# The first group's node work and turn moved from the expert stage into the last attention step

## The chip, the cores and the metric

The kernel runs on one core of one Trainium2 chip. The metric is the device time of one execution in microseconds (us), as the median of several runs; smaller is better. The core has a matrix engine (TensorE, PE in the rows), VectorE (DVE), ScalarE (ACT), GpSimd (POOL) and SyncE (SP), which run side by side and wait for each other through semaphores. SP only issues DMAs here; GpSimd issues the indirect gathers of the attention.

## The reference, cut to what matters

```python
xn = _layernorm(x, axis=-1)                     # 6250 nodes, 256 columns
x = x + relu(gat(xn, edges)) + mix(xn)          # 200000 edges sorted by destination, and a linear attention
x = x + ffn(_layernorm(x, axis=-1))             # 8 experts of three 256x256 layers, router weights w

# gat, for a node: alpha = exp(e - max) / sum, out = sum(alpha * xp[src]) over its edges, 4 heads of 64
# mix, for a node: v + q2 kv / sqrt(N), with q2 divided by its sum and its norm (a reciprocal and a root)
# ffn:
h = relu(bn(xn2 @ W1[e])); h = relu(bn(h @ W2[e])); y[e] = h @ Wo[e] + bo[e]; out = sum_e w[:, e] * y[e]
```

All of it is in float32. Between the two halves stands, for each node, what this text calls the **node work**: divide the sums of the edge attention by their denominator, take the relu, add x and the mix term with its own scale, take mean and variance, normalize. The normalized rows are then turned (transposed), since the experts' products need the columns on the partitions.

## The kernel before

The 6250 nodes lie in 49 blocks of 128, and the blocks in 7 groups of 7 (`IB = 7`). Three stages follow each other, each in an `nc.Block()`, at whose end all engines wait for each other: `prepare`, `attend`, `experts`.

**attend** goes through the edge list in 55 steps of up to 8 visits (the last has 7). A visit is 512 gathered edges with one block of destinations. In a step VectorE first works out the running maxima and the factors of the whole step (a long chain of small instructions, with TensorE turns and small products between), ScalarE takes the exponentials `fo` and `w`, and then the visits run. In visit v VectorE makes `y` (L1300, three quarters of it; ScalarE the fourth, L920), TensorE multiplies it by the one-hot matrix into `ps_y` (L1068), and VectorE scales the running sums `acc` (L1437) and adds `ps_y` (L1442) one visit later. ScalarE widens the one-hot matrix to float32 (L979). Between the visits VectorE builds the one-hot matrices of the next step (L1164); in the last step there is nothing to build, and `first_scales` (nine small instructions) and `first_bases` (x and the mix term of the first group, seven instructions, L1358) stand there. The rows of mix for the first group come by a DMA (`first_in`, L825) that SP issues one step before the end. GpSimd's part of attend ends with the last gather.

**experts** goes through 7 groups and in each through 8 experts. For an expert, TensorE makes two hidden layers (L1598, into `ps_h`, which ScalarE takes out, L1651) and the output (L1608), which VectorE adds up with the router's weight (L1818). The node work of group g+1 runs on VectorE between the experts of group g. The first group has no group before it: its node work, `first_nodes` (L1672 to L1690), stands at the stage's start on VectorE, in two halves, with turns on TensorE (`turns`, L1573) and copies on ScalarE (`turned`, L1632) behind it, and the first hidden layer's products stand behind those. At the stage's start SP issues the loads of the experts' weights (L1545, three of 256 KB for each expert), then `bo`, the router's rows and the mix rows of the second group. TensorE's first hidden product waits for the first expert's three loads.

The order on each engine is the order of the code, which is written out for each engine apart; there is no planner. A semaphore's count is held from one stage to the next, so work that is moved to attend has to raise the counts that experts waits for.

Each of the engines' programs takes its instructions in order: a wait holds up all that stands behind it on that engine.

## Time and profile before

| | us |
|---|---|
| median of 3 runs | 4544.69 (4532.37 to 4567.01) |
| profiled execution | 4539.39, of which the span is 4537.6 |
| attend ends, experts begins (from the span's start) | 3498.3 |
| TensorE busy over the span | 3066.3 (68%) |
| VectorE | 2271.5 (50%) |
| ScalarE | 1537.3 (34%) |
| GpSimd | 1500.8 (33%) |

The times in the rows further down are in us from the span's start. The profiled execution ran 5.3 us below the median of the runs. The stage `experts` takes the last 1039 us of the span, the stage `attend` most of what lies before it. The change touches some 50 us around the border between the two, so the profile is read there, instruction by instruction. Busy time of TensorE is modelled at its ends, and GpSimd's spans are rough.

### The profile page before, as it was taken

Reading aid. Unit: us, or ns where it says so; the run is one execution under the profiler, and the core shown is the slowest. Engines: PE = TensorE matmul, PEld = TensorE weight load, DVE = VectorE, ACT = ScalarE, POOL = GpSimd, SP = SyncE. Lnnn points to the kernel's source line nnn. Section 1 sums busy time; section 2 is a strip of 40 time slices with the busy share of each in tenths; the row PEclk is TensorE's granted clock in tenths of the full one; section 3 lists DMA queues with packets and bytes.
Section 4 is the critical chain, followed back from the end, with each engine's and each line's share of the span. In section 5 each row is a group of like instructions: output and inputs, shape, how many; then the busy total and the mean of one; then the engine's idle time right before and its main releaser. Section 6 shows DMA issues by size and latency. Waiting matters only on the chain. (4 is left out here: it accounts for less than half of the span.)

```text
span 4537.6 us, 61951 instructions
## 1 busy us (share of the span) xinstructions
PE 3066.3 (68%) x18597; PEld 2300.7 (51%) x18597; DVE 2271.5 (50%) x6618; ACT 1537.3 (34%) x4071; POOL 1500.8 (33%) x1622
## 2 busy tenths in 40 slices
PE   6365655565545556665665555555657999999999
PEld 4244544454434455554554444444545666666665
DVE  5154544554544544444444454454547666666653
ACT  3033333333332333333333333333334333333333
POOL 0545444444444444434444343444441000000000
PEclk8577766776766677777777776776767999999999
DMA  6323222322222223322333222222222110101100
GB/s 221 98 73 84 75 79 73 82 76 79 70 74 73 68 82 88 82 77 76 87 82 90 70 71 66 72 75 72 74 73 86 52 33 25 33 9 33 30 11 9
DMA packets 203310, 315.96 MB, mean 70 GB/s; under 512 B 77409, under 2 KB 137442, under 8 KB 202850
## 3 DMA queue, kind: packets, MB, share of 16 engines
q0 software_dynamic: 75360, 212.42, 17.6%
q1 hardware_dynamic: 118722, 90.76, 6.7%
q10 hardware_dynamic: 8896, 8.82, 0.6%
q8 instruction: 151, 2.47, 0.2%
q14 instruction: 181, 1.48, 0.1%
HBM read 279.51 MB, written 26.86 MB: 68 GB/s over the span
## 5 line engine op out<-in xcount | busy, mean ns | idle before, releaser
L768 POOL DMA_INDIRECT xg<-edge_table,idx x1564 | 1485.5, 950 | 1810.1 <-ACT y L920 823.9
L1068 PE MATMUL ps_y<-y,hotw 128*128 128x260 f32 x3512 | 1036.2, 460 | 830.2 <-DVE y L1300 655.9
L1068 PEld LDWEIGHTS ps_y<-y,hotw 128*128 128x128 f32 x3512 | 793.6, 233 | 1048.7 <-ACT hotw L979 677.1
L1442 DVE TENSOR_TENSOR acc<-acc,ps_y 128x260 f32 x439 | 186.8, 425 | 1244.5 <-remote 986.3
L979 ACT CAST hotw<-hot 128x512 f32<-128x512 bf16 x439 | 265.8, 620 | 1041.4 <-remote 701.8
L920 ACT ACTIVATE y<-xg,w 128x65 f32 x1756 | 463.5, 337 | 9.0 <-issue 1.6
L870 ACT COPY hot_t<-ps_o 128x1024 bf16<-128x1024 bf16 x220 | 213.2, 1014 | 652.1 <-remote 486.7
L1300 DVE TENSOR_TENSOR y<-xg,ps_v 128x780 f32<-128x780 f32 x439 | 417.0, 960 | 8.5
L1818 DVE SCALAR_TENSOR_TENSOR xg<-ps_ye,wts,xg 128x256 f32<-128x256 f32 x392 | 189.7, 484 | 400.0 <-PE ps_ye L1608 399.8
L1608 PE MATMUL ps_ye<-wo,xg 128*128 128x256 f32 x1568 | 352.5, 382 | 0.5 <-DVE xg L1818 0.5
L1598 PE MATMUL ps_h<-xg,w 128*128 128x448 f32 x896 | 348.3, 542 | 1.0 <-issue 0.5
L1598 PE MATMUL ps_h<-tables,w 128*128 128x448 f32 x896 | 345.9, 539 | 0.0
L1651 ACT ACTIVATE tables<-ps_h,bnb,bns 128x448 f32<-128x448 f32 x224 | 162.3, 724 | 494.9 <-PE ps_h L1598 494.9
L1608 PEld LDWEIGHTS ps_ye<-wo,xg 128*128 128x128 f32 x1568 | 280.1, 189 | 81.3 <-DVE xg L1818 12.9
L1164 DVE TENSOR_TENSOR hot<-ps_v,tables 128x1024 bf16<-128x1024 f32 x220 | 263.1, 1217 | 0.0
L1598 PEld LDWEIGHTS ps_h<-tables,w 128*128 128x128 f32 x896 | 170.2, 190 | 166.5 <-issue 124.9
L1598 PEld LDWEIGHTS ps_h<-xg,w 128*128 128x128 f32 x896 | 171.0, 191 | 150.9 <-issue 126.9
L1651 ACT ACTIVATE xg<-ps_h,bnb,bns 128x448 f32<-128x448 f32 x224 | 162.3, 724 | 174.5 <-PE ps_h L1598 174.5
L1437 DVE TENSOR_TENSOR acc<-acc,ps_v 128x260 f32 x439 | 182.8, 416 | 0.1
L1051 PE MATMUL ps_fml<-pair,hot_t 128*128 128x8 bf16 x5280 | 147.5, 176 | 41.9 <-ACT hot_t L870 41.9
L1051 PEld LDWEIGHTS ps_fml<-pair,hot_t 128*128 128x128 bf16 x5280 | 147.6, 101 | 46.5 <-ACT hot_t L870 46.5
L1035 PE MATMUL ps_fml<-tail,hot 128*128 128x13 bf16 x1760 | 56.1, 172 | 167.6 <-DVE tail L1222 153.3
(289 smaller groups left out, 3410.5 us busy)
## 6 DMA issues: line engine op xcount, KB each, us to landing
xg<-edge_table,idx POOLq DMA_INDIRECT x1564
mix_rows<-kk SPq DMA_DIRECT2D x49, 257.0 KB
xg<-mix_rows SPq DMA_DIRECT2D x7, 1799.0 KB, 7.9
xb<-in_xt SPq DMA_DIRECT2D x50, 128.0 KB
xnk<-in_x SPq DMA_DIRECT2D x50, 128.0 KB
x<-in_x SPq DMA_DIRECT2D x7, 896.0 KB, 12.4
xt<-in_xt SPq DMA_DIRECT2D x7, 896.0 KB, 9.4
xb<-in_xt SPq DMA_DIRECT2D x24, 256.0 KB
```

The lines of the kernel that those rows point to most:

```text
L768: pool.indirect_dma_start(xg[:, q * OCT + u, j, :], None, dr["table"], bass.IndirectOffsetOnAxis(ap=idx[q][:, c:c + 1], axis=0)).then_inc( ...
L870: act.copy(hot_t[:, 2 * p:2 * p + 2, :].rearrange("p v n -> p (v n)"), ps_o[p % 2][:]).then_inc(ht_d, 1)
L920: mul = act.activation(y[v % 2][:, YV, at], xg[:, bass.ds(slot[v], 1), YV, at].rearrange("p o c -> p (o c)"), ACT.Copy, scale=w[:, v * CH ...
L979: act.copy(hotw[v % 2][:], hot[q][:, v, :, :]).then_inc(hotw_d, 1)
L1051: mm = pe.matmul(ps_l[:, c * 8:c * 8 + 8], hot_t[:, v, j * P:(j + 1) * P], pair[:, k, :, v], start=(k == 0), stop=(k == 2))
L1068: mm = pe.matmul(ps_y[v % 2][:, 0:RW], hotw[v % 2][:, j, :], y[v % 2][:, j, :], start=(j == 0), stop=(j == CH - 1))
L1164: dve.tensor_tensor(hot[q][:, part * k:(part + 1) * k, :, :].rearrange("p v j n -> p (v j) n"), bc(iota, 1, k * CH), bc(rel, 2, P), ALU.is ...
L1300: dve.tensor_tensor(y[v % 2][:, 0:YV].rearrange("p j (h c) -> p j h c", c=HC), xg[:, bass.ds(slot[v], 1), 0:YV, 0:RW].rearrange("p o j (h ...
L1598: mm = pe.matmul(ps_h[g % 4][:, 0:HN], wl[:, kh, e, mh * P:(mh + 1) * P], src[:, kh, half * HN:(half + 1) * HN], start=(kh == 0), stop=(kh ...
L1608: mm = pe.matmul(ps_y[j % 2][:, 0:D], h2[:, kh, j * P:(j + 1) * P], wo[:, kh, e, :], start=(kh == 0), stop=(kh == 1))
L1651: act.activation((h1, h2)[layer][:, mh, half * HN:(half + 1) * HN], ps_h[g % 4][:, 0:HN], ACT.Relu, bias=K.bnb[:, layer, c:c + 1], scale=K ...
L1818: dve.scalar_tensor_tensor(yb[q][:, j, :], ps_y[j % 2][:, 0:D], wts[q][:, j, e:e + 1], yb[q][:, j, :], ALU.mult, ALU.add).then_inc(S["expe ...
```

## The change

The node work of the first group and its turn are moved into the last step of attend and divided anew:

- GpSimd takes, behind its last gather, one product (sums by denominators), the relu, two sums and the product of the mix term, each over all seven blocks at once (128 x 1792), and later the seven normalizations (128 x 256).
- VectorE gives it the reciprocals of the denominators at the step's start, has `first_scales` ahead of the visits' factors instead of in visit 1, loses the seven `first_bases`, and takes the statistics of the seven blocks in visit 3, their variances in visit 4 and the last reciprocal in visit 6.
- ScalarE takes the first root ahead of the exponential `w` and the second in visit 5, and copies the turned rows behind its visits.
- TensorE turns the seven blocks behind its seven visits, into banks of attend.
- `first_nodes`, `turns` and `turned` go from experts. GpSimd raises the counts for them.
- Some buffers change their place in the gather ring, and the small results get a room there.

```diff
@@ gpsimd, behind the last gather
+                for name in ("z_done", "gat_done", "stats_done_e", "aggr_done_e", "zn_done", "node_products", "node_reads"):
+                    pool.sem_inc(K.exp[name], IB)
+                pool.sem_inc(K.exp["den_done"], 1)
+
+                pool.wait_ge(fsh_d, ONE + 1)
+                pool.wait_ge(y_d, ONE + FREE * SV)
+                pool.wait_ge(ya_d, ONE + FREE * SV)
+                x2 = K.yb[0]
+                pool.tensor_tensor(x2.rearrange("p j (h c) -> p j h c", c=HD),
+                                   K.acc[:, 0:IB, 0:RW].rearrange("p j (h c) -> p j h c", c=HC)[:, :, :, 0:HD],
+                                   bc(f_den, 3, HD), ALU.mult).then_inc(fsum_d, 1)
+                pool.wait_ge(fsum_d, ONE + 1)
+                pool.tensor_scalar(x2, x2, 0.0, None, ALU.max).then_inc(fsum_d, 1)
+                pool.wait_ge(fsum_d, ONE + 2)
+                pool.wait_ge(first_in, 16)
+                pool.tensor_tensor(x2, x2, K.t7[:, :, D + 2:MW], ALU.add).then_inc(fsum_d, 1)
+                pool.wait_ge(fq3_d, ONE + 3)
+                pool.tensor_tensor(temp, K.t7[:, :, 0:D], bc(small[:, 5, :], 2, D), ALU.mult).then_inc(fsum_d, 1)
+                pool.wait_ge(fsum_d, ONE + 4)
+                pool.tensor_tensor(x2, x2, temp, ALU.add).then_inc(fsum_d, 1)
+                pool.wait_ge(frs_d, ONE + 1)
+                for j in range(IB):
+                    pool.tensor_scalar(K.x7[:, :, j, :], x2[:, j, :].rearrange("p (k c) -> p k c", c=P), f_mv[:, j, 0:1], f_std[:, j:j + 1],
+                                       ALU.subtract, ALU.mult).then_inc(fzn_d, 1)
@@ scalar, last step, between the exponentials fo and w
+                    if n(1) == NS - 1:
+                        act.wait_ge(first_in, 16)
+                        act.activation(small[:, 2, :].unsqueeze(2), K.t7[:, :, D + 1:D + 2], ACT.Sqrt).then_inc(froot_d, 1)
@@ scalar, in the visits
-                        if v == 0 and n(1) == NS - 1:
-                            act.wait_ge(first_in, 16)
-                            act.activation(small[:, 2, :].unsqueeze(2), K.t7[:, :, D + 1:D + 2], ACT.Sqrt).then_inc(froot_d, 1)
+                        if v == 5 and n(1) == NS - 1:
+                            act.wait_ge(fvar_d, ONE + 1)
+                            act.activation(f_std, f_std, ACT.Sqrt).then_inc(fstd_d, 1)
@@ scalar, behind the steps
+                for j in range(IB):
+                    act.wait_ge(ftn_d, ONE + j + 1)
+                    act.copy(K.zt[0][:, :, j * P:(j + 1) * P], (ps_t, ps_q)[j % 2][:, 0:D].rearrange("p (k n) -> p k n", n=P)).then_inc(fzt_d, 1)
@@ tensor, behind the steps
+                pe.wait_ge(mixc_d, ONE + NB)
+                pe.wait_ge(fmax_d, ONE + NS)
+                for j in range(IB):
+                    pe.wait_ge(fzn_d, ONE + j + 1)
+                    pe.wait_ge(fzt_d, ONE + max(j - 1, 0))
+                    for kh in range(2):
+                        mm = pe.transpose((ps_t, ps_q)[j % 2][:, kh * P:(kh + 1) * P], K.x7[:, kh, j, :], ident)
+                    mm.then_inc(ftn_d, 1)
@@ vector, last step, behind the reading of the running maxima
+                    if n(1) == NS - 1:
+                        dve.reciprocal(f_den.unsqueeze(3), K.acc[:, 0:IB, 0:RW].rearrange("p j (h c) -> p j h c", c=HC)[:, :, :, HD:HC]).then_inc(fsh_d, 1)
@@ vector, ahead of the look-up
                     if n(1) < NS - 1:
                         build(2, *nxt)
+                    else:
+                        first_scales()
@@ vector, in the visits
-                        elif v == 1:
-                            first_scales()
-                            first_bases(0, 3)
-                        elif v == 2 and n(1) == NS - 1:
-                            first_bases(3, 5)
                         elif v == 3 and n(1) == NS - 1:
-                            first_bases(5, IB)
+                            first_stats()
+                        elif v == 4 and n(1) == NS - 1:
+                            first_vars()
+                        elif v == 6 and n(1) == NS - 1:
+                            first_norms()
@@ vector, new functions
+                def first_stats():
+
+                    dve.wait_ge(fsum_d, ONE + 5)
+                    for j in range(IB):
+                        dve.bn_stats(f_stats[:, j, :], K.yb[0][:, j, :]).then_inc(fst_d, 1)
+
+                def first_vars():
+                    dve.wait_ge(fst_d, ONE + IB)
+                    for j in range(IB):
+                        dve.bn_aggr(f_mv[:, j, :], f_stats[:, j, :]).then_inc(fag_d, 1)
+                    dve.wait_ge(fag_d, ONE + IB)
+                    dve.tensor_scalar(f_std.unsqueeze(2), f_mv[:, :, 1:2], LN_EPS, None, ALU.add).then_inc(fvar_d, 1)
+
+                def first_norms():
+                    dve.wait_ge(fstd_d, ONE + 1)
+                    dve.reciprocal(f_std, f_std).then_inc(frs_d, 1)
@@ experts, tensor
-                    if first:
-                        turns(q, t, 0, HALF)
-                    elif e == 0:
+                    if e == 0 and not first:
                         pe.wait_ge(S["turned"], ONE + t(1))
...
-                            if first and layer == 0:
-                                if half == 1:
-                                    turns(q, t, HALF, IB)
-                                pe.wait_ge(S["node_reads"], ONE + (IB if half else HALF))
@@ buffers
-            K.zt = [room((2 + q) * IB * D, 2 * IN_, "p (k n) -> p k n", n=IN_) for q in range(2)]
-            K.h2 = room(4 * IB * D, 2 * IN_, "p (k n) -> p k n", n=IN_)
+            free = NG % RING * CH * TW
+            K.zt = [room(at, 2 * IN_, "p (k n) -> p k n", n=IN_) for at in (free, 3 * IB * D)]
+            K.h2 = room(2 * IB * D, 2 * IN_, "p (k n) -> p k n", n=IN_)
+            K.fr = ring[:, free + 2 * IN_:free + 2 * IN_ + 13 * IB]
```

How the instructions stand on three engines, before and now. Line numbers differ between the two, since lines were added. VectorE in the last step, from the saving of the maxima to visit 3, before (`sc` are the scores, `small_a` the first group's scales, `xg` in L1358 the group's bases):

```order
L1283 TENSOR_TENSOR sc<-asrc,ps_fml 128x128
L1285 SCALAR_TENSOR_TENSOR sc<-sc 128x128
L1287 TENSOR_TENSOR sc<-sc,ps_fml 128x128
L1289 TENSOR_SCALAR sc<-sc 128x128
L1291 COPY ps_v<-fo 128x32
L1293 COPY ps_v<-w 128x128
...
L1352 TENSOR_TENSOR small_a<-small_a 128x7
L1358 SCALAR_TENSOR_TENSOR xg<-xg,small_a 128x256 x3
L1437 ISA
L1437 TENSOR_TENSOR acc<-acc,ps_v 128x260
L1442 TENSOR_TENSOR acc<-acc,ps_y 128x260
```

VectorE there now:

```order
L1398 TENSOR_TENSOR small_a<-small_a 128x7
L1330 TENSOR_TENSOR sc<-asrc,ps_fml 128x128
L1332 SCALAR_TENSOR_TENSOR sc<-sc 128x128
...
L1405 BN_STATS xg<-xg 128x6 x7
L1494 ISA
L1494 TENSOR_TENSOR acc<-acc,ps_v 128x260
L1499 TENSOR_TENSOR acc<-acc,ps_y 128x260
L1347 ISA
L1347 TENSOR_TENSOR y<-xg,ps_v 128x780
L1410 BN_AGGR xg<-xg 128x2 x7
L1412 TENSOR_SCALAR xg<-xg 128x7
```

The scales stand ahead of the scores now, and statistics and variances stand between a visit's `y` and the adding up of the visit before.

ScalarE from the exponential `fo` (L937) to `w` (L944), now:

```order
L937 ACTIVATE fo<-zz 128x32
L940 ACT_TABLE_LOAD
L940 ACTIVATE small_a<-xg 128x7
L944 ACT_TABLE_LOAD
L944 ACTIVATE w<-sc 128x128
```

The root stands between the two exponentials with a table load on either side; before, it stood behind `w` and the first visit's `y`, with one load.

GpSimd from its last gather to its stage's end, now (before, the last gather was followed by the end):

```order
L773 DMA xg<-edge_table,idx 128x264 x4
L794 ISA
L794 TENSOR_TENSOR xg<-acc,xg 128x1792
L798 TENSOR_SCALAR xg<-xg 128x1792
L801 TENSOR_TENSOR xg<-xg 128x1792
L803 TENSOR_TENSOR xg<-xg,small_a 128x1792
L805 TENSOR_TENSOR xg<-xg 128x1792
L808 TENSOR_SCALAR xg<-xg 128x2x128 x7
```

## Rows read from the trace of the kernel before

**Rows 1.** Windows: start:end, length, busy us (instructions) by engine, PEclk, DMA share, GB/s.
```profile
3530.00:4500.00 970.00, 969.47 (x3210) 592.42 (x3209) 574.31 (x1787) 326.28 (x455) 0.00 (x0) 1.00 0.08 22
```

**Rows 2.** Timeline of PE: start, length, line, operation, count, idle before and its releaser.
```profile
3506.34 2.24 PE L1573 MATMUL ps_n<-cst,xg 128*128 128x128 f32 x8 [8.85 <-DVE xg L1690]
3509.09 5.32 PE L1598 MATMUL ps_h<-xg,w 128*128 128x448 f32 x8 [0.51 <-issue]
...
3519.50 6.18 PE L1598 MATMUL ps_h<-tables,w 128*128 128x448 f32 x16
```

**Rows 3.** Timeline of DVE at the end of attend and the start of experts.
```profile
3497.60 0.43 DVE L1442 TENSOR_TENSOR acc<-acc,ps_y 128x260 f32 x1 [0.77 <-PE ps_y L1068]
3498.35 0.33 DVE L1672 RECIPROCAL den<-acc 128x28 f32<-128x28 f32 x1 [0.33 <-PEq L746]
...
3503.83 0.38 DVE L1681 BATCH_NORM_AGGREGATE mv_e<-stats_e 128x2 f32<-128x6 f32 x4
...
3505.78 1.38 DVE L1690 TENSOR_SCALAR xg<-xg,mv_e,small 128x256 f32<-128x256 f32 x4
```

**Rows 4.** Issues by SP, and times to landing of the last load and of L825.
```profile
3462.33 0.38 SPq L825 DMA_DIRECT2D xg<-mix_rows  x1
...
3499.67 0.60 SPq L1545 DMA_DIRECT2D wo<-in_wo  x1
...
wo<-in_wo SPq DMA_DIRECT2D x1, 256.0 KB, 5.5
...
DMA to landing us min/median/max: 7.4/7.4/7.4
```

**Rows 5.** Windows around the border, the granted clock before the DMA share.
```profile
3512.00:3513.00 1.00, 1.00 (x3) 0.38 (x2) 0.00 (x0) 0.55 (x1) 0.00 (x0) 0.50 1.09 347
3513.00:3516.00 3.00, 2.28 (x10) 1.19 (x8) 0.00 (x0) 1.48 (x5) 0.00 (x0) 0.95 1.10 349
```

**Rows 6.** Timeline of DVE in the last step.
```profile
3472.03 0.26 DVE L1232 TENSOR_REDUCE zz<-ps_fml 128x32 f32<-128x96 f32 x1 [1.13 <-PE ps_fml L1035]
...
3474.33 1.38 DVE L1248 TENSOR_SCALAR acc<-st 128x4 f32 x7
3478.26 0.38 DVE L1283 TENSOR_TENSOR sc<-asrc,ps_fml 128x128 f32<-128x128 f32 x1 [2.55 <-PE ps_fml L1051]
...
3480.37 1.84 DVE L1300 TENSOR_TENSOR y<-xg,ps_v 128x780 f32<-128x780 f32 x2
3482.14 0.16 DVE L1335 TENSOR_TENSOR small_a<-rs 128x7 f32<-128x7 f32 x1
...
3484.01 1.28 DVE L1358 SCALAR_TENSOR_TENSOR xg<-xg,small_a 128x256 f32<-128x256 f32 x3
```

**Rows 7.** Timeline of ACT in the last step, and of its first copies in experts.
```profile
3475.96 0.23 ACT L908 ACTIVATE fo<-zz 128x32 f32<-128x32 f32 x1
...
3481.11 1.28 ACT L935 ACT_TABLE_LOAD   x1
...
3507.04 0.80 ACT L1632 COPY xg<-ps_n 128x256 f32<-128x256 f32 x2 [2.38 <-PE ps_n L1573]
```

**Rows 8.** Timeline of DVE in the step before: first y, and the seventh adding up.
```profile
3446.78 1.84 DVE L1300 TENSOR_TENSOR y<-xg,ps_v 128x780 f32<-128x780 f32 x2
...
3462.43 0.43 DVE L1442 TENSOR_TENSOR acc<-acc,ps_y 128x260 f32 x1
```

**Rows 9.** Groups of POOL: line, operation, count, busy us, mean ns, idle before.
```profile
L750 POOL CAST idx<-ix 128x32 int32<-128x32 int16 x49 | 10.9, 222 | 78.0 <-POOLq L111 77.9
...
L246 POOL MEMSET acc<- 128x196 f32 x1 | 0.4, 445 | 0.3 <-POOLq L1924 0.3
```

**Rows 10.** Timeline of POOL: the last gather of the program.
```profile
3417.27 0.95 POOL L768 DMA_INDIRECT xg<-edge_table,idx  x1 [0.30 <-issue]
```

**Rows 11.** Single lines of DVE: count, shortest, median and longest ns, first and last start.
```profile
L1218 DVE TENSOR_TENSOR tails<-tails,tail x55: 291/293/294, 230.9 to 3470.0; 128x128 f32<-128x128 f32 x55
L1289 DVE TENSOR_SCALAR sc<-sc x55: 226/226/228, 241.8 to 3479.3; 128x128 f32<-128x128 f32 x55
```

More of the change, by code:

```diff
@@ L697, in attend @@
          k_d, kb_d, k2_d, kr1_d, kr_d, kn_d, ka_d, kas_d, col_d, one_d, root_d, kv_d, kvs_d, lim_d, rec_d, kv1_d,
-         fq1_d, fq2_d, froot_d, fq3_d, base_d, dg_d) = (K.att[n] for n in ATTEND_COUNTS)
+         fq1_d, fq2_d, froot_d, fq3_d, dg_d,
+         fsh_d, fsum_d, fst_d, fag_d, fvar_d, fstd_d, frs_d, fzn_d, ftn_d, fzt_d) = (K.att[n] for n in ATTEND_COUNTS)
         YV = CH - 1
@@ L1353, in first_scales @@
                     dve.wait_ge(fq3_d, ONE + 3)
-                def first_bases(lo, hi):
-                    for j in range(lo, hi):
-                        dve.scalar_tensor_tensor(K.yb[0][:, j, :], K.t7[:, j, 0:D], small[:, 5, j:j + 1], K.t7[:, j, D + 2:MW],
-                                                 ALU.mult, ALU.add).then_inc(base_d, 1)
+                def first_stats():
[11 more added lines that the diff above has]
+                    dve.reciprocal(f_std, f_std).then_inc(frs_d, 1)
                 def bias(p):
@@ L1614, in _ @@
             def _(act):
-                def product(k, j, t):
-                    act.wait_ge(S["node_products"], ONE + t(NPR) + ((k - 3) * IB + j + 1))
                 def node(k, q, t, before):
@@ L1627, in node @@
                         act.activation(lg[:], lg[:], ACT.Exp).then_inc(S["lg_exp"], 1)
-                def turned(q, t, lo, hi):
-                    for j in range(lo, hi):
-                        product(3, j, t)
-                        act.copy(zt[q][:, :, j * P:(j + 1) * P], ps_n[j % 2][:, 0:D].rearrange("p (k n) -> p k n", n=P)).then_inc(S["node_reads"], 1)
                 def expert(e, q, t):
@@ L1636, in expert @@
                     first = e == 0 and t(1) == 0
-                    if first:
-                        for k, at in enumerate((slice(0, HALF), slice(HALF, IB))):
-                            act.wait_ge(S["half_var"], ONE + k + 1)
-                            act.activation(small[:, 9, at], small[:, 8, at], ACT.Sqrt).then_inc(S["half_std"], 1)
-                            if k == 0:
-                                turned(q, t, 0, HALF)
                     for layer in range(2):
                         for half in range(2):
-                            if first and layer == 0 and half == 1:
-                                turned(q, t, HALF, IB)
                             for mh in range(2):
@@ L1808, in expert @@
                     if e == 0 and t(1) == 0:
-                        first_nodes(q, t)
                         first_weights(q, t)
```

45 lines of the change are left out of this document (7 added, 38 removed).

## The prediction, written before the changed kernel ran

> **What bounds the kernel now.** I began with the windows. Behind 3530 us TensorE is busy for 969.5 of 970 us at full clock [rows 1]: the expert stage is TensorE's, it has no slack, and whatever moves its first products moves the end by the same amount. So the whole question is when TensorE gets through its opening. The timeline of TensorE shows that opening [rows 2]: the visits end at 3497.5, the engine is idle for 8.85 us, turns four blocks, starts on the first hidden layer at 3509.09, stops once more for the other three blocks, and begins the second hidden layer at 3519.50. From there it does not stop for the first group's node work again. I use 3519.50 as the mark: what the second layer's start gains or loses, the kernel gains or loses. VectorE's timeline shows what fills the hole [rows 3]: the stage border at 3498.3, then the node work, whose first normalized blocks come from 3505.8 on.
>
> Two other things are hidden in that hole. The first expert's third load is issued at 3499.67 and takes 5.5 us [rows 4], so it lands at about 3505.2, 6.9 us behind the border. Now nothing waits for it, since the products come at 3509.09. And the granted clock is still 0.50 (1.2 GHz) up to 3513, then 0.95 and full (2.4 GHz) [rows 5]; after the idle stretch it is low for 6.7 us, counted from TensorE's restart at 3506.34.
>
> **What experts saves.** With the first group turned in advance, the first product waits for the weights alone. Loads can't be issued ahead of the border, as their room belongs to experts, so it starts 7.0 us behind it. It saves no more than the time from there. The first layer has 16 products. At the low clock one takes 0.77 us (5 of them in the 3.9 us from 3509.09 to 3513), at full clock 6.18 / 16 = 0.386 us [rows 2]. TensorE is idle for those 7 us again, so I carry the 6.7 us at the low clock over: 8.7 products in them, and 7.3 more in 2.8 us, together 9.5 us. The second layer starts 7.1 + 9.5 = 16.6 us behind the border. Before it was 3519.5 - 3498.3 = 21.2. **Saved: 4.6 us.** With a border later than 3502.9 the change loses.
>
> **What the last step of attend costs.** From front to back:
> - The reciprocal of the denominators takes 0.33 us [rows 3] on VectorE ahead of the scan L1209, on the chain. That chain meets slack at the look-up, which TensorE's own queue holds up (VectorE waits 2.55 us for it ahead of 3478.26).
> - `first_scales` takes 1.9 us (3482.14 to 3484.01) and goes into that wait, which begins at 3475.7 [rows 6]. Its sixth instruction needs the root. ScalarE ends `fo` at 3476.2 [rows 7], loads a table in 1.28 us and has the root at 3477.8; four more instructions end at 3478.6. The scores start at 3478.65, **0.4 us later**. The second table load (1.28 us) fits before `w`, which is due at 3480. Behind ScalarE's new wait for `first_in` stand `w` and all visits, but that DMA is issued at 3462.3 and lands 7.4 us later, at 3469.7 [rows 4], so it holds nothing.
> - Out of the visits go the scales (1.9 us) and the bases (seven at the pitch of L1358, 1.28 us for three, 3.0 us) [rows 6]. The step before shows visits without these. From the first `y` to the seventh adding up 3462.43 - 3446.78 = 15.65 us [rows 8]; in the last step it is 3497.60 - 3480.37 = 17.2 [rows 3, 6]. The builds that stand in that step are covered by TensorE's slow first visit.
> - Into the visits come seven statistics at the pitch of a 128x256 instruction, 0.35 us (1.38 us for 4 of L1690) [rows 3], 2.5 us; seven aggregates and a small one (0.38 us for 4) [rows 3], 1.0 us; a reciprocal, 0.2 us. From visit 2 on the visits run at 1.75 us with VectorE, TensorE and ScalarE all near full, so I count all 3.7. ScalarE's root in visit 5 costs 1.5 us with its table load, ahead of the last widening; I take 0.4 of it as showing, between none and all. The last adding up then starts at 3480.8 + 15.65 + 3.7 + 0.4 = 3500.5, and TensorE ends its visits with it.
> - GpSimd. Its last gather starts at 3417.27 [rows 10], so the count raising and the library's reload lie in 45 us of idleness; at nothing, as long as the reload is shorter. It starts at about 3467, when the denominators are there. No row shows a GpSimd instruction of this kind. Below: VectorE's rate, about 2.1 us for 1792 elements (780 in 0.92) [rows 8]. Above: GpSimd's own slope, (445 - 222) ns over (196 - 32) elements = 1.36 ns each [rows 9], once for each of two inputs, 5.05 us. One input by that slope is 2.6 us. For two I take 3.8, the middle between one pass and two of the engine's own rows. Four of 3.8 and one of 2.6: the first three run from 3467 to 3477.3, the other two from the scales at 3478.7 to 3486.4. VectorE comes to its statistics behind `y` of visit 3, at 3480.8 + 8.1 = 3488.9. So **no wait, with 2.5 us to spare**; at 5.05 us it would wait 1.1 us. Behind that wait stand the scaling and adding of visit 2 and `y` of visit 4, so TensorE would stand too.
> - The normalizations begin at about 3498.2, seven of 0.53 us (0.18 + 256 x 1.36 ns) end at 3501.9, in time for the turns. TensorE's seven turns start at 3500.5 and go at the pitch of the copies, 0.5 us (two in 0.80, and a short wait for the next turn) [rows 7], and the last copy ends at 3504.3. The border is 0.3 us later, at **3504.6**. Nothing is behind these on the three engines but the border itself, for which SP's weight loads wait.
>
> Sum: 3504.6 - 3502.9 = **+1.7 us**. The changed places of the buffers cost nothing; shapes and engines are the same. The mix rows of the second group come behind all weight loads and so 6.3 us later too; ScalarE takes their root ahead of the second expert's results, and TensorE can fill four banks of hidden products (6 us) meanwhile, so a wait of that size does not reach it.
>
> Against the profiled execution that is 4539.4 + 1.7 = 4541.1. The median of the runs lies 5.3 us above the profiled one, and a new median should as well: **4546**.
>
> **The rivals.**
>
> *The two engines share a way to SBUF* and VectorE's instructions with two inputs there wait for a whole GpSimd instruction. For it: in the last step the engines would now work side by side on SBUF for the first time. Against it: L1218 (two inputs in SBUF) took 291 to 294 ns and L1289 226 to 228 in all 55 steps, under gathers or not [rows 11]; but a gather reads little more than indices. Price: L1218, due at 3470.3, waits for the first product to end at 3470.75, the next two for the relu (3473.65) and the sum (3477.7). L1232 then comes at 3479.1 instead of 3472.03 and the scales end at 3484.7. The square of the scores (L1285) waits behind GpSimd's fourth to 3488.6, and L1289 behind the fifth to 3492.7. `y` starts at 3493.8, 13 us later than in my sum. That makes 4554 on the profiled one and **4559** on the median; with only the first half of it, 4551. The Trainium skill, "SBUF — State Buffer", section "Who interferes with whom", says that a VectorE instruction with two SBUF inputs, or in a two-port mode, and a GpSimd instruction that reads SBUF exclude each other for the whole instruction. By that rule, this is what happens.
>
> *GpSimd is at the cheap end* (2.1 us), ScalarE's root is hidden and half of the statistics falls into slack of the visits: the border is at 3502.5, the kernel 0.4 us faster; with a shorter stretch at the low clock 2 to 3 us faster, **4542**. It can't be more, since the weights' landing stands behind the border.
>
> *The library's reload is long*: slower. Place: the row ahead of GpSimd's first product. It decides from about 48 us on, the gap from 3419 to 3467; above that each us holds the statistics, VectorE and TensorE. No row prices it. At 100 us it would add some 54, **4600**. If it is paid instead at the first product, with some us, it adds what goes over the 2.5 to spare, 4 or 5. For that the Trainium skill, "GPSIMD Engine Reference", section "2.1 Instruction dispatch", gives about 6 us for the first call of a freshly loaded kernel; no run here shows it.
>
> **Chances.** My sum 0.42; the shared way, whole or in part, 0.38; the cheap end 0.12; the reload exposed 0.08, of which 0.03 above 45 us. The runs scattered from 4532 to 4567, so a median of a few can lie 10 us off without any change. The range takes in the cheap end less this, and the shared way plus this: 4532 to 4569. A measurement of this kernel tells about 1%, 45 us, from no change. No case but a long reload reaches that: faster by over 1% 0.01, within 0.96, slower 0.03.
>
> **What would show it.** In the changed profile: (1) the border near 3504.6, and the first hidden product 7 us behind it, waiting for a DMA; (2) no wait of VectorE for GpSimd in visit 3, the GpSimd products near 3.8 us; (3) L1218 and its like at 0.29 us, and the scores at 3478.7; if they stretch to the ends of GpSimd's instructions, the rival is right; (4) GpSimd's first product at 3467; (5) the turns at 0.5 us each behind the visits; (6) the first layer in about 9.5 us. Wrong would make it above all (3), and a GpSimd instruction above 5 us.

## The result, and the profile after

| | before | changed |
|---|---|---|
| median of the runs taken in turn, us | 4553.1 (4532.37 to 4567.01, 14 runs) | 4583.66 (4568.44 to 4592.8, 14 runs) |
| profiled execution, us | 4539.39 | 4576.59 |
| its span, us | 4537.6 | 4574.8 |

The ratio is 1.0061, with a 95% interval of 1.0046 to 1.0075: **the kernel became some 30 us slower** (21 to 34 by the interval). Within the 1% that counts here as no change, but outside the predicted range of 4532 to 4569, and 38 us above the predicted 4546. Of these 38, 8.4 are no part of the change: the 14 runs of the kernel before have their median at 4553.1, where the three runs ahead of the prediction had 4544.7.

All comparisons below count from one instruction that stands in every version: the scan `fmax` (`TENSOR_TENSOR_SCAN`) of the last attention step. Up to it the kernels run the same code but for the reciprocals of the denominators (0.32 us on VectorE, just ahead of it), and yet the profiled executions on comparable chips reach it at 3459 to 3484 us, in no order that goes with the edits (before 3466.52, and 3468.32 when profiled again; changed 3479.82; experiment 6 below 3483.91, experiment 8 3459.11). I take that as scatter of the 54 steps ahead, and so 13.3 of the 37.2 us between the two spans; no run shows it apart from a small cost of the change up there. The rest lies behind the scan:

| us behind the scan | before | changed | predicted |
|---|---|---|---|
| first `y` of the visits | 13.85 | 28.27 | 14.3 |
| last adding up starts | 31.08 | 47.00 | 34.0 |
| last copy of the turns ends | (in experts) | 54.52 | 37.8 |
| border (SP's first weight issue) | 31.79 | 62.86 | 38.1 |
| first hidden product | 42.57 | 68.26 | 45.1 |
| second hidden layer (the mark) | 52.98 | 75.89 | 54.7 |

(The predicted column is the prediction's own times less 3466.52.) The mark is 22.9 us later instead of 1.7. Another 0.95 us is lost behind it, and from there to the end nothing: 13.3 + 22.9 + 0.95 = 37.2.

The timeline of VectorE of the changed kernel, last step (start, length, line, operation, count, idle before and its releaser), answers to [rows 6, 11]:

```profile
3479.82 1.19 DVE L1254 TENSOR_TENSOR_SCAN fmax<-seg_step,ps_at 32x512 f32<-32x512 f32 x1
3482.03 0.72 DVE L1259 TENSOR_TENSOR tail<-ps_fml,tables 128x128 bf16<-128x128 f32 x1 [1.02 <-PE ps_fml L1058]
...
3483.09 0.29 DVE L1263 TENSOR_TENSOR tails<-tails,tail 128x128 f32<-128x128 f32 x1
3483.41 4.68 DVE L1265 CAST tail<-tails 128x128 bf16<-128x128 f32 x1
3488.13 3.73 DVE L1267 TENSOR_TENSOR tail<-tails,tail 128x128 bf16<-128x128 f32 x1
...
3499.08 0.17 DVE L1392 TENSOR_TENSOR small_a<-small_a 128x7 f32<-128x7 f32 x1 [1.28 <-ACT small_a L940]
...
3500.34 2.95 DVE L1332 SCALAR_TENSOR_TENSOR sc<-sc 128x128 f32<-128x128 f32 x1
...
3503.65 3.61 DVE L1336 TENSOR_SCALAR sc<-sc 128x128 f32<-128x128 f32 x1
...
3508.09 1.84 DVE L1347 TENSOR_TENSOR y<-xg,ps_v 128x780 f32<-128x780 f32 x2
...
3526.82 0.43 DVE L1499 TENSOR_TENSOR acc<-acc,ps_y 128x260 f32 x1 [0.77 <-PE ps_y L1103]
```

And GpSimd's own timeline beside it, whole from its last gather on:

```profile
3479.96 3.19 POOL L794 TENSOR_TENSOR xg<-acc,xg 128x1792 f32<-128x1792 f32 x1 [45.05 <-DVE xg L1247]
3483.24 4.74 POOL L798 TENSOR_SCALAR xg<-xg 128x1792 f32<-128x1792 f32 x1
3488.07 3.61 POOL L801 TENSOR_TENSOR xg<-xg 128x1792 f32<-128x1792 f32 x1
3499.97 3.18 POOL L803 TENSOR_TENSOR xg<-xg,small_a 128x1792 f32<-128x1792 f32 x1 [8.29 <-DVE small_a L1398]
3503.23 3.96 POOL L805 TENSOR_TENSOR xg<-xg 128x1792 f32<-128x1792 f32 x1
3524.75 8.44 POOL L808 TENSOR_SCALAR xg<-xg 128x256 f32<-128x256 f32 x7 [17.56 <-DVE xg L1416]
```

Lay the two over each other. L1265 starts 0.17 us behind the start of GpSimd's L798 and ends with it, at 3488.0 to 3488.1; L1267 ends with L801; L1332 with L803; L1336 (L1289 of before, 226 ns in all 55 steps there) with L805. Nobody is named as releaser: the time is inside the instruction. L1263 (L1218 of before), which starts 0.06 us before L794 ends and runs across the gap of 0.09 us to L798, keeps its 0.29, and L1259, which reads one input from PSUM, runs at 0.72 in the middle of L794. L1265, L1267 and L1332 are L1220, L1222 and L1285 of before, where they took, in all 55 steps (count, shortest/median/longest ns, first and last start):

```profile
L1220 DVE CAST tail<-tails x55: 245/249/316, 231.3 to 3470.3; 128x128 bf16<-128x128 f32 x55
L1222 DVE TENSOR_TENSOR tail<-tails,tail x55: 316/319/327, 231.5 to 3470.6; 128x128 bf16<-128x128 f32 x55
L1285 DVE SCALAR_TENSOR_TENSOR sc<-sc x55: 291/291/294, 241.1 to 3478.7; 128x128 f32<-128x128 f32 x55
```

The turns, on TensorE, and what stands behind them; answers to [rows 2]:

```profile
3526.55 0.38 PE L1190 MATMUL ps_at<-cst,xg 128*128 128x128 f32 x2
...
3533.25 0.69 PE L1190 MATMUL ps_at<-cst,xg 128*128 128x128 f32 x2 [0.51 <-POOL xg L808]
3548.08 7.79 PE L1640 MATMUL ps_h<-xg,w 128*128 128x448 f32 x16 [14.14 <-DMA wo<-in_wo]
3555.71 6.18 PE L1640 MATMUL ps_h<-tables,w 128*128 128x448 f32 x16
3561.73 3.19 PE L1621 MATMUL ps_n<-wr,xg 128*128 128x8 f32 x28
3564.77 8.02 PE L1650 MATMUL ps_ye<-wo,xg 128*128 128x256 f32 x28
3572.63 6.18 PE L1640 MATMUL ps_h<-xg,w 128*128 128x448 f32 x16
```

ScalarE's last copy:

```profile
3533.97 0.37 ACT L1024 COPY xg<-ps_at 128x256 f32<-128x256 f32 x1 [0.83 <-PE ps_at L1190]
```

SP's first issues behind the border; they answer to [rows 4]:

```profile
3542.68 1.31 SPq L1601 DMA_DIRECT2D w<-in_w  x2
3544.05 1.07 SPq L1601 DMA_DIRECT2D wo<-in_wo  x1
```

Between 3534.3, where the last copy ends, and 3542.68 no engine shows any work. The view of the single line that ends the stage names the one that is not done. Of the changed kernel, GpSimd and the engine that works last (count, shortest/median/longest ns, first and last start):

```profile
L751 POOLq DRAIN  x1: 17419/17419/17419, 3524.7 to 3524.7; - x1
L751 ACTq DRAIN  x1: 401/401/401, 3534.0 to 3534.0; - x1
```

The same view of the kernel before:

```profile
L746 POOLq DRAIN  x1: 8879/8879/8879, 3424.3 to 3424.3; - x1
```

At the end of a stage each engine has a row called DRAIN, and the border comes when the last of these has ended; I call it the engine's emptying, after its name. GpSimd's starts with its normalizations and lasts until 3542.1, 8.9 us behind the end of the last of them (3533.2). In the kernel before a DRAIN of 8.88 us stood at 3424.3, behind the last gather, and ended 65 us ahead of the border.

### The profile page after: what moved, and what is told of

It reads as the page before. It is cut to its first block and busy times, and to the rows that moved or that the text cites. A ratio compares the mean times of both kernels' runs of the same rounds, so it can differ in the third digit from the quotient of the medians.

```text
span 4574.8 us, 61952 instructions
## 1 busy us (share of the span) xinstructions
PE 3065.1 (67%) x18597; PEld 2302.1 (50%) x18597; DVE 2274.0 (50%) x6588; ACT 1540.6 (34%) x4072; POOL 1527.6 (33%) x1634
## 5 line engine op out<-in xcount | busy, mean ns | idle before, releaser
L1086 PE MATMUL ps_fml<-pair,hot_t 128*128 128x8 bf16 x5280 | 147.7, 175 | 45.1 <-ACT hot_t L899 41.8
L1799 DVE SCALAR_TENSOR_TENSOR xg<-bo,wts,xg 128x256 f32<-128x256 f32 x392 | 160.1, 480 | 3.6
```

What stands on the lines that cost most here:

```text
L1086: mm = pe.matmul(ps_l[:, c * 8:c * 8 + 8], hot_t[:, v, j * P:(j + 1) * P], pair[:, k, :, v], start=(k == 0), stop=(k == 2))
```

## The experiments

**The theory (A)**: three things, each with its place, make the loss behind the scan. (1) VectorE's instructions that need the way to SBUF which GpSimd uses wait for whole GpSimd operations, and ScalarE's root moves in behind them; (2) GpSimd normalizes at 1.21 us a block, so the turns follow it; (3) GpSimd's DRAIN costs about 9 us behind its last instruction. **The rival (B)** differs by experiment: the two engines slow each other by sharing a rate, whatever the size of the operations (2); the DRAIN costs its 9 us each time, or because of the computing ahead of it (1, 4, 8); part of the loss sits in the regrouped work itself, beside the weights and the clock (6). That a semaphore orders the wait is a fourth, which 2 can tell as well.

The first four runs fell on a chip that takes 3203.4 us for the kernel before; its steps of attention are shorter. Each has its own comparison there, the kernel before was timed there but not profiled, and the offsets from the scan are what is compared with the table above.

**1. GpSimd emptied early.** The changed kernel, with one line more:

```diff
@@ gpsimd, behind the counts raised for experts
+                pool.drain()
```

> The changed kernel with one drain more on GpSimd, right behind its last gather, where the engine is idle anyway; the one at the stage's end stays. The mark is the stretch from the scan of the last step (32x512) to the start of the first expert's second hidden layer: 53.0 us before, 75.9 us changed. In the changed kernel 8.3 us of it lie between the last copy of a turned block and SP's first weight load, while GpSimd's closing drain runs. Theory A (the drain works off what the gathers left, once, whenever it comes): the closing drain falls from 8.9 us behind GpSimd's last instruction to under 0.5 us, the border follows the last copy by about 0.3 us, the mark falls to 67.6 us and the time by about 8 us. Theory B (GpSimd's drain costs 9 us each time, or costs it because of the computing instructions ahead of it): the early drain shows 9 us in idleness, the closing one 9 us again, the mark stays at 76.

Measured: 3222.53 us, ratio 1.0058 (1.0041 to 1.0075). The view of the new line:

```profile
L790 POOLq DRAIN  x1: 8883/8883/8883, 2122.3 to 2122.3; - x1
```

The row that changes GpSimd's configuration, and its first product:

```profile
L795 POOLq MODIFY_POOL_CONFIG  x2: 11/11/11, 2131.3 to 2131.3; - x2
```

```profile
2131.45 3.19 POOL L795 TENSOR_TENSOR xg<-acc,xg 128x1792 f32<-128x1792 f32 x1 [15.95 <-issue]
```

ScalarE's last copy:

```profile
2187.06 0.37 ACT L1025 COPY xg<-ps_at 128x256 f32<-128x256 f32 x1 [0.83 <-PE ps_at L1191]
```

SP's first weight issue:

```profile
2187.72 1.31 SPq L1602 DMA_DIRECT2D w<-in_w  x2
```

The border comes 0.66 us behind the start of the last copy; in the changed kernel it was 8.71. So (3) holds, and a second DRAIN with no gather since the first is short: it ends 0.1 us behind the last normalization. But the mark is at 72.1, not at 67.6: on this chip the early DRAIN ends at 2131.2, 1.9 us *behind* the scan, the first product starts 2 us late, and one more of VectorE's instructions (L1264 there, 2.19 us instead of 0.29) falls into it; first `y` is 2.2 us later than in the changed kernel. The visits take 1.4 us more, for which this trace names no reason, and the weights 0.8 more. An emptying in front of due work is no gift: it took 8.1 us off the border, and the mark gained 3.8.

**2. GpSimd's long operations in pieces.** The five operations of 128x1792 become seven of 128x256 each, the rest of the changed kernel the same:

```diff
-                pool.tensor_scalar(x2, x2, 0.0, None, ALU.max).then_inc(fsum_d, 1)
+                for j in range(IB):
+                    op = pool.tensor_scalar(x2[:, j, :], x2[:, j, :], 0.0, None, ALU.max)
+                op.then_inc(fsum_d, 1)
...
```

(shown for the maximum with zero; the other four operations likewise.)

> The changed kernel with each of GpSimd's five instructions of 128x1792 cut into seven of 128x256, block by block. Theory A (a VectorE instruction that needs the shared way to SBUF waits for the whole GpSimd instruction that holds it): the stretched VectorE instructions (cast of the tails 4.68 us, the next 3.73, square of the scores 2.95, minimum of the scores 3.61) fall to at most about 1 us each, more of them are stretched a little, and the way from the scan to the first y falls from 28.3 us to about 17 to 20 (13.9 before). Theory B (the two engines slow each other by sharing bandwidth, whatever the size of the instructions): the stretched instructions stay as long in sum, some 15 us over their lengths of before, and the way stays near 28 us. GpSimd's sum may grow by some us of overhead, from 18.7 to 20 to 25.

Measured, one execution (3221.0 us): first `y` at 17.77, last adding up at 35.92, the mark at 66.7. VectorE's timeline of this kernel, the instructions that had stretched:

```profile
2137.28 0.54 DVE L1275 CAST tail<-tails 128x128 bf16<-128x128 f32 x1
2137.86 0.53 DVE L1277 TENSOR_TENSOR tail<-tails,tail 128x128 bf16<-128x128 f32 x1
...
2143.08 3.20 DVE L1303 TENSOR_SCALAR acc<-st 128x4 f32 x7
...
2149.44 0.39 DVE L1342 SCALAR_TENSOR_TENSOR sc<-sc 128x128 f32<-128x128 f32 x1
```

4.68 us became 0.54, 3.73 became 0.53, 2.95 became 0.39, and the last, 3.61, became 0.23: VectorE still waits, but for the rest of a piece of 0.6 to 0.8 us. GpSimd works no less (23.3 us for the five against 18.7), its semaphores rise at the same places, and `y` comes 10.5 us earlier. So it is (1): a shared rate, or a wait for a semaphore, would have cost as much with pieces. What is left, 3.9 us to the kernel before, is made of many small waits: seven short savings (L1303) take 3.20 us where they took 1.39.

**3. The normalizations on VectorE**, behind its last adding up, the rest of the changed kernel the same:

```diff
@@ gpsimd
-                for j in range(IB):
-                    pool.tensor_scalar(K.x7[:, :, j, :], x2[:, j, :].rearrange("p (k c) -> p k c", c=P), f_mv[:, j, 0:1], f_std[:, j:j + 1],
-                                       ALU.subtract, ALU.mult).then_inc(fzn_d, 1)
@@ vector, behind the visits
+                dve.wait_ge(frs_d, ONE + 1)
+                for j in range(IB):
+                    dve.tensor_scalar(K.x7[:, :, j, :], K.yb[0][:, j, :].rearrange("p (k c) -> p k c", c=P), f_mv[:, j, 0:1], f_std[:, j:j + 1],
+                                      ALU.subtract, ALU.mult).then_inc(fzn_d, 1)
```

> The changed kernel with the seven normalizations (128x256) on VectorE, behind its last adding up, in place of GpSimd's 1.21 us each. VectorE takes 0.35 us each (2.4 us). GpSimd's last instruction is then the second sum, at the end of the scores, so that its closing drain of 9 us lies beside the visits. Expected if both readings are right: from the last adding up to the border 2.4 + 0.8 + 0.3 = 3.5 to 4.5 us instead of 15.9, the mark 75.9 - 12 = 64 us. If the drain's length were set by the border and not by GpSimd's last instruction, the border would still come 9 us late and the mark would be 72.

Measured, one execution (3218.3 us): VectorE needs 2.34 us for the seven where GpSimd needed 8.44:

```profile
2179.39 2.34 DVE L1512 TENSOR_SCALAR xg<-xg 128x256 f32<-128x256 f32 x7
```

The border is 5.0 us behind the start of the last adding up instead of 15.9 (3.5 to 4.5 were expected), the mark at 64.8. Two causes went with one edit: the last copy came 2.8 us sooner behind the last adding up (2), and as GpSimd now ended with its fifth operation, its DRAIN lay beside the visits (3): it ends 8.9 us behind that operation and 15 us ahead of the border. The first `y` stayed at 28.0, as nothing of (1) was touched.

**4. One late instruction in the kernel before.** The reverse test of (3): nothing of the change, only a fill of one column on GpSimd that waits for the last but one adding up.

```diff
+                pool.wait_ge(acc_d, ONE + NG + NX - 1)
+                pool.memset(late[:], 0.0).then_inc(late_d, 1)
```

> The kernel before with nothing but one GpSimd memset of 128x1 more, that waits for the last but one adding up of the last step. Theory A (GpSimd's closing drain takes 9 us from its last instruction on, whatever that is, once gathers have run in the stage): the border comes about 8 us later than before, the mark rises from 53.0 to 61 us, the time by 8 us (0.2%). Theory B (only the reloaded library or the long computing instructions make the drain slow): the mark stays at 53.

Measured: 3211.11 us, ratio 1.0021 (1.0012 to 1.0031). On GpSimd's timeline:

```profile
2157.97 0.10 POOL L783 MEMSET late<- 128x1 f32 x1 [43.56 <-DVE acc L1445]
```

And on SP's:

```profile
2167.23 1.31 SPq L1548 DMA_DIRECT2D w<-in_w  x2
```

With a fill of 0.10 us the border stands 38.5 us behind the scan instead of 31.8, and from the fill's end to the border pass 9.2 us. It costs some 7 us of the kernel (0.21% of 3203), as the trace says (mark 60.0 against 53.0). The 31.8 and 53.0 are from the other chip; as the first `y` is 0.6 us earlier in this trace, the true step is perhaps that much larger.

**5. The kernel before, profiled again** on the chip of this run and the next three, where the kernel before takes about what it took in the first runs (4541.1 us here), to see how firm the offsets are:

> The kernel before, unchanged, on the chip of this call: a measure of how much of the marks is the chip's and the run's. Both theories expect the last step to take what it took in the trace shown (first y 13.9 us behind the scan, last add 31.1, first weight issue 31.8, second layer of the first expert 53.0), within 1 us, whatever the earlier steps take.

First `y` 13.79, last adding up 31.00, border 31.71, mark 52.93: all within 0.1 us of the first trace, while the scan itself stood 1.8 us elsewhere.

**6. All three suspects gone at once**: experiments 1, 2 and 3 in one kernel.

> The changed kernel with all three suspects taken away at once: GpSimd's five long operations in seven pieces each, its closing drain preceded by one behind the last gather, and the seven normalizations on VectorE behind its last add. Theory A (the loss is whole GpSimd operations held against VectorE, the normalizations on GpSimd, and the closing drain, and nothing else): first y at 17.8 us behind the scan, or up to 2 us more where the early drain ends after the scan; last add at 36 to 38; first weight issue 4.5 to 5 us behind the last add; second layer at 53 to 56 us behind the scan, where the kernel before has 53.0: a ratio of 1.000 to 1.001. Theory B (part of the loss is in the regrouped work itself, beside the experts' weights and the clock): these three gone, the mark stays at 58 us or more and the ratio at 1.0015 or more.

Measured: 4549.01 us, ratio 1.0007 (0.9989 to 1.0025). First `y` 17.73, last adding up 36.11, border 41.11, mark 54.41. Theory A's numbers, one by one. The mark is 1.4 us behind that of before: the three are the loss (21.5 of the 22.9 us), and without them the change still buys nothing. The border costs 9.3 us more (3.9 for pieces that still hold VectorE, 1.2 for the statistics in the visits, 4.3 for normalizing and turning behind them), and the experts give 7.9 back.

**7. A version meant to beat both**, from the kernel before. GpSimd keeps the sums, with its one-input operation given to ScalarE; what needs the shared way longest stands beside the visits, whose instructions on VectorE read one input from PSUM; statistics, normalizations and turns stay behind the border, where the weights are awaited anyway:

```diff
@@ gpsimd, behind its last gather
+                pool.drain()
+                pool.wait_ge(fsh_d, ONE + 1)
...
+                pool.tensor_tensor(x2..., K.acc..., bc(f_den, 3, HD), ALU.mult).then_inc(fsum_d, 1)
+                pool.wait_ge(fsum_d, ONE + 2)
...
+                pool.wait_ge(fq3_d, ONE + 3)
+                pool.tensor_tensor(x2, x2, K.t7[:, :, D + 2:MW], ALU.add).then_inc(fsum_d, 1)
+                pool.tensor_tensor(temp, K.t7[:, :, 0:D], bc(small[:, 5, :], 2, D), ALU.mult).then_inc(fsum_d, 1)
+                pool.wait_ge(fsum_d, ONE + 4)
+                pool.tensor_tensor(x2, x2, temp, ALU.add).then_inc(fsum_d, 1)
@@ scalar, last step
+                        act.wait_ge(fsum_d, ONE + 1)
+                        act.activation(K.yb[0]..., K.yb[0]..., ACT.Relu).then_inc(fsum_d, 1)
@@ vector, visits
-                            first_bases(0, 3)
...
@@ vector, first_nodes of experts
-                        dve.scalar_tensor_tensor(yb[q][:, j, :], q7[:, j, :], 0.0, yb[q][:, j, :], ALU.max, ALU.add).then_inc(S["z_done"], 1)
```

> A version meant to beat both: from the kernel before, with the node sums of the first group on GpSimd but without its long one-input operation (one product of 1792 columns at the scan, the maximum with zero on ScalarE in its idle time, three more operations beside VectorE's visits), the early drain behind the last gather, and only statistics, variances, normalizations and turns left behind the border, where the weights take 5 to 7 us to land anyway. Theory A: first y 14 to 15 us behind the scan, visits 1.5 us shorter than before, border at 30 to 32 us, second layer at 46 to 49 us against 53.0 before: 4 to 7 us gained, a ratio of 0.998 to 0.9988 here. Theory B (the three GpSimd operations beside the visits hold VectorE's products up as they held the tails, about 3 us each): border at 38 or more, and no gain.

Measured: 4536.04 us, ratio 0.9989 (0.9974 to 1.0004). First `y` 13.66, last adding up 29.60, border 30.31, mark 46.89. GpSimd's timeline:

```profile
3477.61 3.18 POOL L792 TENSOR_TENSOR xg<-acc,xg 128x1792 f32<-128x1792 f32 x1 [48.74 <-DVE xg L1228]
3494.91 3.62 POOL L798 TENSOR_TENSOR xg<-xg 128x1792 f32<-128x1792 f32 x1 [14.11 <-DVE small_a L1373]
3498.49 3.18 POOL L799 TENSOR_TENSOR xg<-xg,small_a 128x1792 f32<-128x1792 f32 x1
3501.74 4.02 POOL L801 TENSOR_TENSOR xg<-xg 128x1792 f32<-128x1792 f32 x1
```

VectorE's timeline beside it:

```profile
3496.46 0.96 DVE L1326 TENSOR_TENSOR y<-xg,ps_v 128x780 f32<-128x780 f32 x1
3497.34 0.42 DVE L1458 TENSOR_TENSOR acc<-acc,ps_v 128x260 f32 x1
3498.30 0.43 DVE L1463 TENSOR_TENSOR acc<-acc,ps_y 128x260 f32 x1 [0.55 <-PE ps_y L1092]
```

10.8 us of GpSimd beside the visits, and `y` keeps its 0.96 us, the adding up its 0.42: theory B's price of 3 us an operation is not paid. The closing DRAIN ends 0.1 us behind the last sum. The mark is 6.1 us earlier than before, the largest gain that the trace of any version shows.

**8. The same without its early DRAIN.**

> The version above without its early drain, all else the same. Theory A: GpSimd's last operation ends about 14 us behind first y, at 28 to 30 us behind the scan; its closing drain then takes about 9 us and ends at 37 to 39, so the border comes 6 to 8 us later than in the version with the early drain and the second layer at 53 to 56 us. If the early drain ends after the scan and holds GpSimd's first product up, this version's first y comes up to 2 us earlier. Theory B (the closing drain doesn't depend on the earlier one in this kernel): both versions have the same border.

Measured: 4543.53 us, ratio 1.0007 (0.9992 to 1.0022); border 37.44, mark 53.82. GpSimd's last operation starts at 3483.39 and takes 4.01 us, and the stage's end says:

```profile
L749 POOLq DRAIN  x1: 12953/12953/12953, 3483.4 to 3483.4; - x1
```

It ends at 3496.35, 8.95 us behind the operation. The first `y` is at 13.66 in both, so the early DRAIN, which ends 33 us ahead of the scan on this chip, costs nothing. That one instruction is worth 6.9 us at the mark.

**9. The version of 7 once more**, for its interval:

> The version that beats both by its trace, once more, since five rounds left its interval over 1 (0.9974 to 1.0004). Theory A: its second layer 6 us earlier behind the scan is kept to the end: a ratio of about 0.9985 (0.998 to 0.999), interval mostly under 1. Theory B (the gain is given back later, as a colder clock in the experts or a later transfer): 1.000.

Measured: 4494.94 us, before 4496.54 in the same runs, ratio 0.9994 (0.998 to 1.0007); mark 46.75. The trace's gain is there each time, the time of the whole doesn't prove it: both intervals reach over 1. It is not given back in large part. From the first `ps_ye` product to the end of the span pass 1010.0 us in it, as in the changed kernel, and 1009.0 in the kernel before, so 6.1 us at the mark are 5.1 at the end, 0.11%, less than the scatter of such runs lets one see. The ratio hoped for, 0.998 to 0.999, was missed by its middle value, so that this version beats the kernel before is not shown. Against the changed kernel it is faster without doubt, 0.7% between the ratios (0.9989 and 0.9994 against 1.0061, whose intervals lie far apart).

## Why the prediction was wrong

By its own steps, in us; the differences in the right column add up to the mark's, 21.2, but for rounding.

| step | predicted | measured | difference |
|---|---|---|---|
| scan to first `y` (reciprocal, scales, root) | 14.3 | 28.27 | +14.0 |
| visits, first `y` to last adding up | 19.7 | 18.7 | -1.0 |
| last adding up to the end of the last copy | 3.8 | 7.5 | +3.7 |
| from there to the border | 0.3 | 8.3 | +8.0 |
| border to second layer | 16.6 | 13.0 | -3.6 |

**"The scores start at 3478.65, 0.4 us later": failed, and it was the failure of principle.** The rival of the shared way to SBUF was right, as test (3) of the prediction had said it would show: the like of L1218 stretch to the ends of GpSimd's instructions. The scores started 20.1 us behind the scan (L1330 at 3499.93), where 12.1 were predicted. The rival's price of 13 us for `y` was nearly right (14.0 measured against the sum, 14.4 against before), though it had the operations at 3.8 and 2.6 us, and held L1218, which slipped through a gap. The prediction gave it 0.38 and the sum 0.42 on rows of 291 to 294 and 226 to 228 ns that never had a GpSimd *arithmetic* operation beside them [rows 11]; such rows can't speak against it.

The Trainium skill, "SBUF — State Buffer", section "Who interferes with whom", states this rule, and adds that a cast or `tensor_scalar` can fall under it through a two-port mode, while a VectorE instruction with at most one SBUF input outside such a mode does not. The runs agree on each count: L1265 and L1336, one input each, held for 4.68 and 3.61 us; L1259 (0.72 us) and the visits of experiment 7 (0.96 and 0.42), with one input from PSUM, not held.

The root was mis-sized too. ScalarE had `fo` only at 3497.22, as the look-up's products came late with everything else, and its table load (1.28 us) lay open: VectorE waited 1.28 us (L1392), where the scales had been meant to go into TensorE's queue. Once the cover was late, so was what it covered.

**"The border is 0.3 us later": failed.** It was read from a border at which GpSimd had long been done. The prediction said of the turns and copies: "Nothing is behind these on the three engines but the border itself". The price was in the trace of before, in the view of the line that ends the stage (8.88 us at 3424.3), hidden by the 65 us of idleness behind it. The prediction named for every moved part the cover it gets and left out that GpSimd's own *ending* lost its cover by working until the border. No rival had it, so even the rival that was right put the mark some 8 us too early (54.7 and 13, 67.7 against 75.9; its other misses, +1.0, -1.0, +3.7 and -3.6, cancel). Experiments 1, 4 and 8 each show it alone: 8.0, 6.7 and 7.1 us of border.

**"seven of 0.53 us", GpSimd's normalizations: failed by size.** 1.21 us each. The slope of a fill and of a cast (1.36 ns an element) [rows 9] does not hold for an operation with two scalars a partition (4.7 ns). TensorE's turns wait 0.3 to 0.76 us for each. The long two-input operations, taken at 3.8 between bounds of 2.1 and 5.05, were right (3.18 to 3.96); the maximum with zero, one input, at 2.6, was the slowest of them with 4.74.

**The visits** were right within a microsecond: 18.7, and VectorE did not wait for the sums in visit 3.

**"Saved: 4.6 us" in experts: right in kind, mis-sized by 3.6 us in the change's favour.** The first product waits for `wo`, as predicted, but it starts 4.0 us after that load's issue and 5.4 after the border instead of 7.0 (5.5 us from issue in [rows 4]). And from it to the second layer pass 7.6 us instead of 9.5: the granted clock was at 0.50 (1.2 GHz) only for the first 3 us of them, not for the 6.7 that were carried over, as these windows show (columns as in [rows 1]; they answer to [rows 5]):

```profile
3548.00:3551.00 3.00, 2.92 (x4) 1.51 (x5) 0.00 (x0) 0.00 (x0) 0.00 (x0) 0.50 0.88 272
3551.00:3555.00 4.00, 4.00 (x12) 1.94 (x11) 0.00 (x0) 2.04 (x3) 0.00 (x0) 0.98 0.99 371
3575.00:4545.00 970.00, 970.00 (x3203) 591.10 (x3202) 572.26 (x1780) 328.27 (x459) 0.00 (x0) 1.00 0.08 21
```

The last of them bears out the prediction's first reading: behind the opening nothing moves. But the opening is longer than was thought. The windows behind 3564.8 (TensorE's busy time alone, and the clock) show what the 0.95 us behind the mark are:

```profile
3564.80:3566.80 2.00, 2.00 (x7) 0.50 1.10 347
3566.80:3568.80 2.00, 2.00 (x7) 0.64 1.10 348
3568.80:3570.80 2.00, 2.00 (x11) 1.00 1.01 312
```

From the first of the 28 `ps_ye` products to the second expert pass 7.9 us, some 3 of them at 0.50 (1.2 GHz), with TensorE busy all the while; in the kernel before 6.9 us, a wait of 0.5 us among them, at full clock throughout. The same second dip, and the same 1.0 us, is in every version whose first products come sooner behind the border, also in the one of experiment 7 (1010.0 against 1009.0 us from there to the end). Why the clock falls a second time was not settled. What the engine did just before are the router's 28 products of 8 columns (L1621, 3.2 us, still at full clock), and the weights of the next experts stream (the DMA share, 1.10); but the kernel before has the same 28 products ahead of its `ps_ye`, at a share of 1.06, and no fall behind them.

**What was right and did not matter:** the reload of GpSimd's code, put at nothing, cost nothing that shows: the row that changes its configuration is 11 ns, and the first product starts 0.14 us behind the scan's start. The Trainium skill, "GPSIMD Engine Reference", section "2.1 Instruction dispatch", gives about 6 us for the first call of a freshly loaded kernel. In the changed kernel the idleness ahead of the first product could hide such a gap; in experiment 1, where the configuration changes at 2131.3, straight behind the DRAIN, and the product starts at 2131.45, there is none.

**The whole.** On the mark and behind it the trace explains 22.9 + 0.95 = 23.9 us. The runs say 30.5, with an interval of 21 to 34. So the sum lies inside it, but some us between them are scatter or something ahead of the scan that no run here tells apart from it. On the quicker chip experiment 1 agrees closer: 19.1 us at the mark, if the kernel before has it at 53 there too (an estimate), 20 with the tail, and 18.6 measured (13 to 24).

## What to carry to other kernels

Before work goes to an idle GpSimd, list what VectorE does at that moment: instructions with two SBUF inputs, and casts or scalings between SBUF tiles, stop for the whole of each GpSimd operation, while those that read one input from PSUM run on. So put the long operations beside the latter, or cut them. And look up what the engine's emptying at the stage's end takes; if gathers went before, an early emptying in idle time made it short here, and without it one late instruction, however small, puts it on the path. Last, what is awaited at a border anyway (weights, here 5 us) is a cheap place for work: the statistics, normalizations and turns that experiment 6 has ahead of the border cost some 6.7 us there (2.4 in the visits, 4.3 behind them) and gave 3.3 back behind it, against experiment 7. That is an estimate, as the two kernels differ in more than this.

## What the runs showed of the hardware that was not expected

- GpSimd's DRAIN at the end of the stage of 1564 gathers takes 8.9 us, alone (8879, 8883 ns) or behind the last operation (17419 and 12953 ns in all), even 44 to 98 us after the last gather; the next one, with no gather between, ends 0.1 us behind the last operation. It need not be the same everywhere: in the first stage, with four gathers, the DRAIN (9117 ns from 30.3) ends 5.6 us behind the end of the last of them (33.8). What sets its length was not tried.
- GpSimd's operations do not follow the number of inputs: 128x1792 in 3.18 us with a factor spread along the columns, 3.61 to 4.02 for a plain sum, and 4.74 for the one-input maximum with a constant (4.83 from its start to the next one's). Cut in seven they are longer in sum, 23.3 against 18.7 us.
- VectorE's seven short savings of 128x4 (L1293 of the changed kernel, 1.39 us) take 3.20 us beside GpSimd's pieces, some 0.26 more each: small instructions pay often for the rest of a piece.
